# A gated graph layer and eight routed experts on one core: the expert loop with a longer lag between its stages, rings of more buffers, and passes that empty in between

## The reference, cut to what matters

```python
def reference(x, adj, ...):                       # x: 128 graphs x 128 nodes x 128 features
    x = x + gnn(layernorm(x), adj, adj, ...)      # first stage
    x = x + ffn(layernorm(x), Wg, bg, W1, b1, W2, b2)   # second stage

def gnn(h, adj_in, adj_out, ...):
    msg_in = (einsum('mn,bnd->bmd', origin * adj_in, h) + edge_bias) * sigmoid(h @ gate + bias)
    msg_out = (einsum('mn,bnd->bmd', origin.T * adj_out, h) + out_edge_bias) * sigmoid(...)
    return relu(msg_in + msg_out + h * sigmoid(h @ loop_gate))

def ffn(x, Wg, bg, W1, b1, W2, b2):               # 16384 tokens, 8 experts, hidden width 512
    top_w, top_i = top_k(x @ Wg + bg, 2)          # two experts for each token
    for e in range(8):
        h = gelu(x @ W1[e] + b1[e])
        out = out + w_dense[:, e:e + 1] * (h @ W2[e] + b2[e])
```

## Time and profile before

| | us |
|---|---|
| median of 3 runs | 772.68 |
| the runs | 769.83 to 773.42 |
| the profiled execution's own time | 766.71 |
| its span, first to last instruction | 764.9 |

### The profile page before, as it was taken

How to read it: one execution, slowest core, us unless ns; L and a number is a source line. 1 busy time by engine, 2 the same in 40 slices (tenths; PEclk the granted TensorE clock), 3 DMA queues, 4 the chain that set the end, 5 groups by cost and what they waited for, 6 DMA issues and landing times.

```text
span 764.9 us, 18892 instructions
## 1 busy us (share of the span) xinstructions
PE 689.8 (90%) x5004; PEld 627.9 (82%) x5004; DVE 625.5 (82%) x2129; ACT 515.6 (67%) x1389; POOL 501.9 (66%) x460
## 2 busy tenths in 40 slices
PE   3879999799997549999998999999999999999991
PEld 2557677577675439999998999998999999999990
DVE  5989986889989648888888788887888888888881
ACT  3888878478875326676776677776677777777770
POOL 1534656365665774655678578886888888888883
PEclk9997977578887559999999999999999999999996
DMA  8465878463522266578857867459764543544310
GB/s 255 145 203 159 287 261 97 80 140 106 208 92 76 98 189 187 180 216 285 254 169 242 258 176 192 129 173 359 225 170 127 140 126 99 152 124 126 86 43 15
DMA packets 100336, 127.07 MB, mean 166 GB/s; under 512 B 37367, under 2 KB 61824, under 8 KB 100240
## 3 DMA queue, kind: packets, MB, share of 16 engines
q1 hardware_dynamic: 81600, 83.41, 39.4%
q0 software_dynamic: 17344, 42.51, 16.6%
q10 hardware_dynamic: 1296, 0.14, 0.2%
HBM read 71.41 MB, written 56.99 MB: 168 GB/s over the span
## 4 chain that ended last, share of the span: by engine, by line
PE 50%; DMA 4%; issue 1%; POOL 1%; SPq 0%; POOLq 0%; DVE 0%
PE bank L1262 7%; PE bank L1264 7%; PE bank L1263 7%; PE bank L1276 7%; PE bank L1277 7%; PE bank L1281 7%; DMA w_t<-w_split 4%; PE bank L1290 3%; PE bank L1252 3%; POOL out_dram L645 1%; SPq L482 0%; POOLq L151 0%; SPq L466 0%; DVE row L1137 0%; SPq L476 0%
## 5 line engine op out<-in xcount | busy, mean ns | idle before, releaser
L767 ACT ACTIVATE act_f<-bank,b_t 128x256 f32<-128x256 f32 x560 | 220.0, 476 | 42.6 <-PE bank L1264 41.8
L645 POOL DMA_INDIRECT out_dram<-row,to_row x140 | 182.0, 1300 | 47.6 <-issue 36.3
L648 POOL DMA_INDIRECT rows<-row,to_row x140 | 162.5, 1160 | 76.5 <-DVE row L1137 46.7
L610 POOL DMA_INDIRECT rows<-row,slot_low x128 | 131.3, 1026 | 93.2 <-DVE row L833 58.1
L1125 DVE TENSOR_TENSOR act_lo<-act_f,act_hi 128x1024 fp32r<-128x1024 f32 x140 | 170.3, 1216 | 0.1
L1262 PE MATMUL bank<-in_hi,w_t 128*128 128x256 f32 x560 | 158.1, 282 | 4.0 <-DMA w_t<-w_split 4.0
L1264 PE MATMUL bank<-in_hi,w_t 128*128 128x256 f32 x560 | 157.3, 281 | 0.0
L1263 PE MATMUL bank<-in_lo,w_t 128*128 128x256 f32 x560 | 156.8, 280 | 0.0
L1276 PE MATMUL bank<-act_hi,w_t 128*128 128x256 f32 x560 | 149.6, 301 | 1.5 <-DMA w_t<-w_split 1.3
L1277 PE MATMUL bank<-act_hi,w_t 128*128 128x256 f32 x560 | 137.5, 280 | 0.0
L775 ACT ACTIVATE y_t<-bank,b_t 128x256 f32<-128x256 f32 x140 | 66.7, 476 | 99.8 <-PE bank L1281 99.8
(11 more groups left out here) (173 smaller groups left out, 1239.3 us busy)
## 6 DMA issues: line engine op xcount, KB each, us to landing
row<-rows SPq DMA_DIRECT2D x140, 260.0 KB, 2.9
w_t<-w_split SPq DMA_DIRECT2D x40, 512.0 KB, 5.2
xs<-in_x_dram SPq DMA_DIRECT2D x16, 512.0 KB, 4.4
rows<-ends_rep SPq DMA_DIRECT2D x14, 260.0 KB, 5.1
b_t<-biases SPq DMA_DIRECT2D x140, 2.5 KB
rows<-row,to_row POOLq DMA_INDIRECT x140
out_dram<-row,to_row POOLq DMA_INDIRECT x140
row<-in_L_ffn_W_dram SPq DMA_DIRECT2D x4, 512.0 KB, 9.7
```

The source lines that it names most:

```text
L610: pool.indirect_dma_start(out=rows, out_offset=bass.IndirectOffsetOnAxis(ap=slot_low[:, r, b:b + 1], axis=0), in_=row[:, r, b, :], in_offs ...
L645: pool.indirect_dma_start(out=out_rows, out_offset=at, in_=got[:, g, j, P:2 * P], in_offset=None, bounds_check=TOKENS - 1, oob_is_err=Fals ...
L648: pool.indirect_dma_start(out=rows, out_offset=at, in_=got[:, g, j, :], in_offset=None, bounds_check=NROWS - 1, oob_is_err=False).then_inc ...
L767: last = act.activation(act_f[:, s, c, :], ps_h[s][:, c, :], ACT.Gelu, bias=b_t[:, w, c:c + 1])
```

## The change

The change sets the second stage's distances anew. layer2 comes two steps behind layer1 (LATE), so the casts of the hidden values have three buffers. unit_back comes five steps behind (BACK), unit_turned three ahead (IN). The hidden values rotate by halves over three PSUM banks, the turned rows and the outputs share three others. The order in a step is the same for PE but for these distances; ACT and DVE change theirs. The loops are written out in full, and each pass runs empty before the next begins. SP's order in a step is not changed, nor are WR, AHEAD and GR.

In the first stage `row` has five slots, the biases are issued right behind the first weights instead of behind chunks 9 and 10, and the last four chunks' scatters have semaphores of their own, which POOL hands on to SP (s_land). EARLY for the second pass is 12.

```diff
-    EARLY = 2 * AHEAD
+    EARLY = [2 * AHEAD, 3 * AHEAD]
+    IN, BACK = 3, 5
+    LATE = 2
+    RING = 5
...
-        row = sb("row", [P, 4, G, ROW])
+        row = sb("row", [P, RING, G, ROW])
...
             for k in range(4, E):
                 load_w(k)
+            biases(0, E)
...
 (DVE, first stage)
-                    wait_slot(dve, s_row, 16 * G, two, 0)
+                    left = two.index - RING
+                    if left >= 0:
+                        dve.wait_ge(s_row[left % 4], 16 * G * (left // 4 + 1))
...
 (DVE, second stage)
             def hidden_hi(t):
-                wait_turn(dve, s_mm2, 1, t, -1)
+                wait_turn(dve, s_mm2, 1, t, -LATE)
...
-            def step(t, second):
-                sum_up(t.back(2), second)
-                hidden_hi(t)
-                tile_lo(t.on(2))
-                hidden_lo(t)
+            for p in range(PASSES):
+                units = of_pass(p)
+                for k in units[:IN - 1]:
+                    tile_lo(unit(k))
+                for k in units:
+                    if k - BACK - 1 in units:
+                        sum_up(unit(k - BACK - 1))
+                    if k + IN - 1 in units:
+                        tile_lo(unit(k + IN - 1))
+                    hidden_hi(unit(k))
+                    hidden_lo(unit(k))
+                for k in units[-BACK - 1:]:
+                    sum_up(unit(k))
...
 (PE)
             def unit_turned(t):
-                    wait_turn(pe, s_inlo, 1, t, 0)
+                if t.index - IN in units:
+                    wait_turn(pe, s_done, 1, t, -IN - BACK if t.index - IN - BACK > units[0] else units[0] - t.index)
+                elif units[0] > 0:
+                    outputs = [k for k in range(units[0]) if bank_of_outputs(k) == bank_of_rows(t.index)]
+                    pe.wait_ge(s_done, outputs[-1] + 1)
...
-            def step(t):
-                layer1(t)
-                unit_back(t.back(2))
-                unit_turned(t.on(2))
-                layer2(t.back(1))
+            for p in range(PASSES):
+                units = of_pass(p)
+                for k in units[:IN]:
+                    unit_turned(unit(k))
+                for k in units:
+                    layer1(unit(k))
+                    if k - BACK in units:
+                        unit_back(unit(k - BACK))
+                    if k - LATE in units:
+                        layer2(unit(k - LATE))
+                    if k + IN in units:
+                        unit_turned(unit(k + IN))
+                for k in units[-BACK:-LATE]:
+                    unit_back(unit(k))
+                for k in units[-LATE:]:
+                    layer2(unit(k))
+                for k in units[-LATE:]:
+                    unit_back(unit(k))
```

More of the change, by code:

```diff
@@ L65, in wait_slot @@
     wait_turn(eng, sems[s], each, Turn(turn.group, (turn.step - s) // ring, turn.unroll // ring, 0), more)
-def turns(eng, unroll, total, body, spans):
-    k = 0
-    for first, last in spans:
-        while k < first * unroll:
-            body(Turn(k // unroll, k % unroll, unroll, total))
-            k += 1
-        with eng.Fori(first, last) as g:
-            for s in range(unroll):
-                body(Turn(g, s, unroll, total))
-        k = last * unroll
-    return k
-def wait_apart(eng, holds, sem, each, turn, more):
-    value = turn.group * (each * turn.unroll) + (each * turn.step + more)
-    if isinstance(value, int):
-        eng.wait_ge(sem, value)
-    else:
-        eng.to_reg(value)
-        eng.wait_ge(holds, 1)
-        eng.wait_ge(sem, value)
 class Own:
@@ L414, in _ @@
                 store_lo(k)
+            with nc.allow_non_contiguous_dma(reason="biases, once"):
+                sp.dma_start(b_dram[:, :, FC], b2).then_inc(s_bias, 16)
             load_x(chunk_of(5))
@@ L864, in turn @@
                 if one.real:
-                    sums(0, one, xs, G // 2)
-                    last = sums(0, one, xs, G // 2 + 2)
+                    sums(0, xs[:, one.slot(4)], G // 2)
+                    last = sums(0, xs[:, one.slot(4)], G // 2 + 2)
                     if not two.real:
@@ L871, in turn @@
                     for b in range(0, G, 2):
-                        last = sums(1, two, row[:, :, :, P:2 * P], b)
+                        last = sums(1, row[:, two.index % RING, :, P:2 * P], b)
                     summed = own(last)
@@ L1061, in _ @@
             own.sync()
-            first, rows_of, seg, lim, at, start = (unit[:, i] for i in range(6))
+            first, rows_of, seg, lim, at, start = (unit_at_[:, i] for i in range(6))
             own(dve.scalar_tensor_tensor(out=change[:], in0=expert[:, 2], scalar=1.0, in1=expert[:, 0], op0=ALU.max, op1=ALU.not_equal))
@@ L1246, in unit_turned @@
             def unit_turned(t):
-                if t.real:
-                    g = t.slot(GR)
-                    wait_slot(pe, s_got, 16, t, 16)
-                    wait_turn(pe, s_inlo, 1, t, 0)
-                    for j in range(BLK):
-                        last = pe.transpose(ps_x[:, j * P:(j + 1) * P], got[:, g, j, 0:P], ident[:])
-                    last.then_inc(s_xt, 1)
+                g = t.slot(GR)
+                wait_slot(pe, s_got, 16, t, 16)
+                units = of_pass(t.index // NU)
@@ L1299, in _ @@
-            for k in range(2):
-                unit_turned(unit_at(k))
-            pe.wait_ge(s_slot, CHUNKS)
-            k = turns(pe, UT, UNITS, step, UNIT_SPANS)
-            for k in range(k, UNITS):
-                step(unit_at(k))
-            last = unit_at(UNITS - 1)
-            unit_back(last.back(1))
-            layer2(last)
-            unit_back(last)
+                for half in range(2):
+                    wait_turn(pe, s_act, 2, t, half - 2)
+                    for i in range(2):
+                        c = 2 * half + i
+                        hi, lo = (w1_t[:, w, k, c * P:(c + 1) * P] for k in range(2))
+                        dst = ps_h(t, half)[:, i, :]
+                        pe.matmul(dst, hi, in_hi[:, s], start=True, stop=False)
+                        pe.matmul(dst, hi, in_lo[:, s], start=False, stop=False)
+                        last = pe.matmul(dst, lo, in_hi[:, s], start=False, stop=True)
+                    last.then_inc(s_mm1, 1)
@@ new lines, in layer2 @@
+            def layer2(t):
+                s, w = t.slot(LATE + 1), t.slot(WR)
+                wait_slot(pe, s_w2, 16, t, 16)
+                wait_turn(pe, s_hhi, 1, t, 1)
+                wait_turn(pe, s_y, 1, t, -1)
+                for c in range(FC):
+                    hi, lo = (w2_t[:, w, k, c * P:(c + 1) * P] for k in range(2))
+                    pe.matmul(ps_y(t), hi, act_hi[:, s, c, :], start=(c == 0), stop=False)
+                    pe.matmul(ps_y(t), lo, act_hi[:, s, c, :], start=False, stop=False)
+                wait_turn(pe, s_hlo, 1, t, 1)
+                for c in range(FC):
+                    hi = w2_t[:, w, 0, c * P:(c + 1) * P]
+                    last = pe.matmul(ps_y(t), hi, act_lo[:, s, c, :], start=False, stop=(c == FC - 1))
+                last.then_inc(s_mm2, 1)
```

274 lines of the change are left out of this document (124 added, 150 removed).

## The result

The changed kernel takes 805.48 us in the median of 4 runs (798.74 to 809.44), the kernel before 771.25 beside it: a ratio of 1.0437, interval 1.0356 to 1.0518. The profiled execution took 805.13, its span is 803.1, so it lies at the median; before it was 764.9. The slowdown is 38.2 us in the spans, where the forecast had 16.1. 789 (776 to 803) was too low; the sign was right.

What follows compares the result with a forecast made beforehand. PE's own work was taken to bound the steady stretch. The terms -12 - 1.5 + 8.7 + 3.6 + 11.6 + 5.7 = +16.1 gave 782.8 us for the profiled run, 789 as a median, range 776 to 803.

Steps and rivals of the forecast that it cites:

- What bounds it, steady pace: Second stage: the steady stretch is bound by PE's own work, 3.248 us a unit, which distances between stages can't shorten.
- First stage and fill, -12 and -1.5: Before layer1(0): a fifth slot of `row` saves 12 us of 13.4 waited; three turnings without two waits save 1.5.
- DVE turns nearly all of it into time: First stage: of the 13.4 us that DVE waits for slots of `row`, 12 come back as time.
- the biases move the wait: First stage, rival: chunk 4 arrives 8.6 us late behind the biases, the gain is 3.4 instead of 12, 797.5; chance 0.07.
- My argument against it: First stage: chunk 4's load is issued when a line of chunk 0 is done, and DVE needs it only next turn.
- Changes of expert, first pass, +8.7: Units 12 to 41: rows behind layer 2's weights on SP come late and stall PE; 15.3 us after, 6.6 before.
- before's surplus: First pass, kernel before: 6.6 us by which layer2's last matmuls stand further apart than 3.248 us around changes of expert.
- Boundary and second pass, +3.6 and +11.6: Emptying between passes stops PE for 3.6 us; units 70 to 77 stall for weights, 14.3 us against 2.7 before.
- the first stall, at layer1(72): Second pass's refill: weights asked for only when layer1(70) is done, so PE stalls 3.75 us.
- The end, +5.7: Behind the last layer1: POOL scatters six units at 2.56 us each and ends at 761.2 instead of 755.5.
- The clock, rival at +12: Second stage: some nine stalls of 2 to 3.5 us are each followed by half clock, 1.3 us each, 801; chance 0.12.
- The loads are covered after all: Rival: rows and weights land early enough to swallow today's 9.3 us surplus, -13.5, 759; 0.12 shared with half-size stalls.

Runs made afterwards that it cites:

- LATE = 1: The changed kernel with layer2 one step behind layer1 instead of two, nothing else: 783.24 us, ratio 1.015 to the kernel before.
- work in the waits: The changed kernel with ten useless matmuls on PE ahead of each of 14 long waits: 798.68 us, ratio 1.036 to the kernel before.

## Right and wrong, step by step

- **What bounds it, steady pace**: right. 25 + 61 units at before's pace.
- **First stage and fill, -12 and -1.5**: wrong, and the largest miss (13.3 of 22.1). The step that failed is "DVE turns nearly all of it into time", with the biases put at no cost for chunk 4. Of the 12, 1.5 came. Of the missing 10.5, 7.2 are the rival "the biases move the wait", whose price was 8.6, and it came as written: chunk 4 landed 17.2 us after its issue behind the biases, before 3.7. My argument against it was right about the issue (33.25, before 33.57) and left out the landing. 1.9 are the short waits: I had counted 3.4 for them, and their turns gave 1.5. I had seen turns without a wait as long as turns with one, less the wait, and took that for a law of DVE; PE was busy nearly all of the turn besides. 1.4 lie in other turns and in the tables behind them; no run takes them apart. The last 2.8 of the 13.3 are the fill: +1.3 instead of -1.5, since a third load of rows must land.
- **Changes of expert, first pass, +8.7**: right in mechanism and place, too small (+14.5). With LATE = 1, 12.6 of it are gone. The stalls had the right size: the waits for rows and weights that the profile lists for PE from unit 12 to 69 are 14.5, where I had 15.3 in all. What failed is the rest of the sum. I took off all 6.6 of before's surplus, but only 4.4 of it are listed waits, so that the waits grew by 10.1. And the clock was at nothing; it has the remaining 4.4 or most of them: 3.0 by work in the waits, 4.1 at most by PE's busy time at half clock, 4.3 between the two profiles with and without a fall. The split between the two is argued from these sums, not measured.
- **Boundary and second pass, +3.6 and +11.6**: 18.2 for 15.2, near in part by luck. PE's stops at unit_back are 1.7 and 0.34 for 1.9 and 0.7. But the first stall, at layer1(72), is 1.9 for 3.75, and PE's listed waits from unit 69 on are 11.6 where I had 17.9; the clock, which I had left out, made up for some of it (3.4 by work in the waits, 6.4 at most). And the two terms aren't causes that could be undone one by one: without the emptying a wait of 6.2 for rows appears.
- **The end, +5.7**: right, +7.9 - 2.3 = +5.6. (The sign for it, POOL's last scatter 18 to 19 us behind the last layer1, should have read 21: 18.9 was counted from before's last layer1. It is 21.1.)
- **The clock, rival at +12**: true in kind, 6 to 9 in size by the times, 10.5 at most. It fell behind five waits, not nine. The Trainium skill (TensorE: Matmul & The Clock Gate, section "HAM oscillation — how this bites in real kernels") has waits for DMA, of 3 to 5 us in its example, put the clock back each time. Here waits of 1.5 to 2.0 us were enough (1.52 at 425.13), but not each time (1.99 at 366), and two executions of one kernel lost the clock in different places.
- **The loads are covered after all**: wrong, and so its 759.
- **The range.** The clock (+7) and the biases (+8.6) came together: 789 + 7 + 8.6 = 804.6. I gave each a chance of its own, as if only one could come, and neither was in the forecast. That this sum meets 805.5 so closely is luck: between the profiles it gives 31.7, and 38.2 was measured. The profiled execution of before had been 6.0 below its median, that of the changed kernel was not.

## What to carry over

- If a stage is moved by a step, write down for each engine's queue, the one that issues DMAs too, which wait the move delays and what stands behind it. Here LATE moved and SP's order didn't, and the waits for rows that came of it went away with either (LATE = 1 gave 24 us; what SP's order alone gives was seen only on the slower chips).
- A wait on one engine is worth its length only if no other engine is within a few per cent of the same turn. Look at every engine's busy time in a single turn before counting it.
- Where a load comes late, compare its issue and its landing in both kernels before you name a cause. Here the issue was 0.3 us earlier and the landing 13 us later.
- Rivals that don't exclude each other belong into one sum. Their chances add up to a range that reaches their joint case.

## What was not expected of the hardware

- Useless matmuls in waits of 1 to 2.3 us kept the granted clock at 1.00 from 286 us to the last unit and made the kernel 7 to 9 us quicker by the medians, 6.4 in the trace. On the slower chips the clock fell in two profiles of the same kernel.
- A load of 512 KB that was issued right behind eight loads of single values (2 KB each) took 17.2 us to land, 3.7 without them. In the kernel with late biases the load of chunk 11, issued ahead of four of them, was waited for until 17.9 us after its issue.
- Issuing eight loads of single values took SP 11.1 us early in the kernel (21.68), 4.9 of it for one of them; four took 3.11 at 116.19 in the kernel before and 10.92 at 127.56 with five slots and late biases. What this depends on was not tested.
- Two of the chips run the same kernel before at 849 to 856 us instead of 771. In the variants' profiles from there layer1(0) stands 37 to 47 us later than in before's on a usual chip.
